# Attention behind a mixture of experts: the first batch's maxima are transposed twice, and plain scores run five slots ahead instead of nine

## What is computed

```python
xn = _layernorm(x)
x = x + attention(xn) + moe(xn)          # B=8, S=256, E=256

# attention: 16 heads of 16, with rotary q and k
scores = jnp.einsum('bshd,bthd->bhst', q, k) / jnp.sqrt(D)
scores = jnp.where(causal, -jnp.inf, scores)
attn = jax.nn.softmax(scores, axis=-1)
out = jnp.einsum('bhst,bthd->bshd', attn, v).reshape(B, S, E) @ Wo + bo

# moe: 64 experts, the best 6 of each token, and 2 shared ones
routed = jnp.einsum('tef,ehf->th', silu(g) * u * comb, w_down)
```

## Time and profile before

| | us |
|---|---|
| Runs of the kernel before, three | 647.65, 649.49, 653.19 |
| Their median | 649.49 |
| The profiled execution | 650.96 |
| Span of its trace, first to last instruction | 649.1 |
| TensorE busy, share of the span | 615.3, 95% |
| VectorE / ScalarE / GpSimd busy | 430.5 / 307.2 / 321.0 |

### The profile page before, as it was taken

How to read it: one execution, slowest core, us unless ns; L and a number is a source line. 1 busy time by engine, 2 the same in 40 slices (tenths; PEclk the granted TensorE clock), 3 DMA queues, 4 the chain that set the end, 5 groups by cost and what they waited for, 6 DMA issues and landing times.

```text
span 649.1 us, 17796 instructions
## 1 busy us (share of the span) xinstructions
PE 615.3 (95%) x4929; PEld 364.3 (56%) x4929; DVE 430.5 (66%) x1366; ACT 307.2 (47%) x802; POOL 321.0 (49%) x340
## 2 busy tenths in 40 slices
PE   6999999998998999998999999999999899999987
PEld 3644455654554555554555555555554566666654
DVE  6768688557664665667665565544446788899865
ACT  3643131033443444444444544444445777777752
POOL 4000000268636775567765686564300776766662
PEclk9999999999997999999999999999999999999999
DMA  9610011138978768996799977996425777777432
GB/s 297 179 30 2 0 34 34 57 103 255 283 228 278 232 190 247 320 334 185 213 298 295 315 222 235 327 327 134 102 59 193 210 232 229 227 227 232 129 109 74
DMA packets 78167, 124.52 MB, mean 192 GB/s; under 512 B 11113, under 2 KB 52618, under 8 KB 78090
## 3 DMA queue, kind: packets, MB, share of 16 engines
q1 hardware_dynamic: 43098, 60.18, 30.4%
q0 software_dynamic: 15872, 46.16, 24.4%
q10 hardware_dynamic: 19120, 17.18, 7.8%
HBM read 85.73 MB, written 37.75 MB: 190 GB/s over the span
## 4 chain that ended last, share of the span: by engine, by line
PE 80%; DVE 6%; DMA 3%; issue 3%; ACT 3%; POOL 2%; DVEq 1%; SPq 0%; ACTq 0%; POOLq 0%
PE pair L1216 23%; PE pair L1243 14%; PE pair L1186 6%; PE pair L1173 5%; PE pair L1121 4%; PE bank L1227 4%; PE bank L1330 4%; PE bank L1200 3%; PE bank L1362 2%; PE pair L1083 2%; DVE negm L985 2%; DMA lower<-xn_rows,idx_all 2%; PE pair L1292 2%; PE pair L1312 1%; PE bank L1341 1%
## 5 line engine op out<-in xcount | busy, mean ns | idle before, releaser
L454 POOL DMA_INDIRECT lower<-xn_rows,idx_all x128 | 138.0, 1078 | 221.8 <-DVE idx_all L958 107.8
L1216 PE MATMUL pair<-space,work 128*64 (+1 forms) x768 | 167.4, 467 | 6.3 <-DVE wqkv_sb L932 3.7
L1243 PE MATMUL pair<-lower,work 88*64 x512 | 121.5, 379 | 0.7 <-ACT lower L615 0.7
L1216 PEld LDWEIGHTS pair<-space,work 128*64 128x64 f32 x768 | 67.4, 138 | 78.4 <-issue 66.9
L874 DVE TENSOR_TENSOR work<-work,pair 128x176 f32<-128x176 f32 x128 | 42.9, 337 | 101.5 <-ACT work L609 100.7
L1243 PEld LDWEIGHTS pair<-lower,work 88*64 88x64 f32 x512 | 69.6, 137 | 48.7 <-issue 18.0
L1216 PE MATMUL pair<-wqkv_sb,work 128*64 128x352 f32 x256 | 90.6, 477 | 0.0
L615 ACT ACTIVATE lower<-pair 128x256 f32<-128x256 f32 x128 | 49.1, 384 | 76.5 <-PE pair L1243 76.5
L519 POOL DMA_INDIRECT wqkv_sb<-y_rows,slot_i x48 | 48.1, 1002 | 58.2 <-DVE negm L985 33.2
L602 ACT ACTIVATE work<-pair 128x256 f32<-128x256 f32 x128 | 42.6, 381 | 66.9 <-PE pair L1173 41.3
L985 DVE TENSOR_REDUCE negm<-pair 128x2 f32<-128x256 f32 (+1 forms) x128 | 64.6, 549 | 9.5 <-PE pair L1292 7.5
(11 more groups left out here) (205 smaller groups left out, 1156.5 us busy)
## 6 DMA issues: line engine op xcount, KB each, us to landing
space<-wgu SPq DMA_DIRECT2D x66, 352.0 KB
y_rows<-lower ACTq DMA_DIRECT2D x128, 128.0 KB, 4.3
qk_all<-qk_rows SPq DMA_DIRECT2D x64, 256.0 KB
lower<-wdn SPq DMA_DIRECT2D x64, 176.0 KB
qk_rows<-qk_all POOLq DMA_DIRECT2D x32, 256.0 KB, 5.7
qk_rows<-space POOLq DMA_DIRECT2D x16, 256.0 KB, 4.0
xn_rows<-qk_all SPq DMA_DIRECT2D x16, 128.0 KB, 1.9
lower<-xn_rows,idx_all POOLq DMA_INDIRECT x128
```

What stands on the lines that cost most here:

```text
L454: po.indirect_dma_start(xg[:, r % XB, :], None, xn_rows[:, :], bass.IndirectOffsetOnAxis(idx_all[:, r:r + 1], 0)).then_inc(xg_in[r % XB], 16)
L1216: last = pe.matmul(pair[u % 2][strip, 0:2 * F], xgT[u][:, c, strip], n, start=c == 0, stop=c == EC - 1, skip_group_check=True)
L1243: last = pe.matmul(pair[u % 2][strip, 512:512 + E], hT[:, u % 2, c, strip], n, start=c == 0, stop=c == 1, skip_group_check=True)
```

## The change

A new constant EARLY = 5. Plain scores run five slots ahead of slot 0; slots 0 to 3 make two each, and from slot 4 on the distance is AHEAD = 9 as before. Ring copies run two further ahead than the scores, and follow the same pattern. The first batch's maxima are turned twice: version 0 of mT holds those of pairs 0 to 3 and serves slots 0 to 3; version 1, made in slots 1 to 3, holds all eight and serves slots 4 to 7; later batches' versions are numbered one higher. halves(0) stands behind the maxima of pair 3, halves(1) behind those of pair 7. negm is cleared at the start. POOL's rows and the constants AHEAD, FILL and LATER are as before.

```diff
+EARLY = 5
+        def scored_at(n):
+            if n < 0:
+                return range(max(n + EARLY, 0), n + EARLY + 1)
+            return range(EARLY + 2 * n, EARLY + 2 * n + 2) if n < EARLY - 1 else range(n + AHEAD, min(n + AHEAD + 1, NS))
+        def ringed_at(n):
+            if n < 0:
+                return range(max(n + EARLY + 2, 0), n + EARLY + 3)
+            return range(EARLY + 2 + 2 * n, EARLY + 4 + 2 * n) if n < EARLY - 1 else range(n + FILL, min(n + FILL + 1, NS))
+        def version_at(n):
+            if n == EARLY - 2:
+                return 1
+            return 0 if n == -1 else (n + 1) // 8 + 1 if n % 8 == 7 and 0 < (n + 1) // 8 < B else None
+        def version_of(n):
+            return n // PAIRS_OF_HEADS + 1 if n >= EARLY - 1 else 0
...
             def a_slot(n):
                 if 0 <= n < NS:
                     exps(n)
-                if n % 8 == 7 and 0 <= (n + 1) // 8 < B:
-                    mT_copy((n + 1) // 8)
+                if version_at(n) is not None:
+                    mT_copy(version_at(n))
                 if n % 8 == 7 and 0 <= (n - 3) // 2 < QUADS:
                     raw_copy((n - 3) // 2)
-                if 0 <= n + FILL < NS:
-                    ring_copy(n + FILL)
+                for f in ringed_at(n):
+                    ring_copy(f)
...
             def d_slot(n):
-                if 0 <= n + AHEAD < NS:
-                    maxes(n + AHEAD)
+                for m in scored_at(n):
+                    maxes(m)
+                    if m == EARLY - 2:
+                        halves(0)
+                    elif m == PAIRS_OF_HEADS - 1:
+                        halves(1)
...
-                if n % 8 == 6 and 0 <= (n + 2) // 8 < B:
-                    halves((n + 2) // 8)
+                if n > 0 and n % 8 == 6 and (n + 2) // 8 < B:
+                    halves((n + 2) // 8 + 1)
...
             dve.memset(npad[:], 0.0)
+            dve.memset(negm[:], 0.0)
...
             def p_slot(n):
-                if 0 <= n + AHEAD < NS:
-                    score_masks(n + AHEAD)
+                early = scored_at(n)
+                for m in early[:1]:
+                    score_masks(m)
                     if n < 0:
-                        keep_on(bank[2][:], 3 if n + AHEAD == 0 else 1)
-                    scores(n + AHEAD)
+                        keep_on(bank[2][:], 3 if m == 0 else 1)
+                    scores(m)
                 if 0 <= n < NS:
                     turned_masks(n)
                     if n == 0:
                         keep_on(bank[2][:], 4)
                     turned_scores(n)
+                for m in early[1:]:
+                    score_masks(m)
+                    scores(m)
```

More of the change, by code:

```diff
@@ L981, in maxes @@
                 dve.wait_ge(s_ok, m + 1)
-                if m and m % PAIRS_OF_HEADS == 0:
-                    dve.wait_ge(npad_ok, m // PAIRS_OF_HEADS)
+                if m == EARLY - 1:
+                    dve.wait_ge(npad_ok, 1)
+                elif m and m % PAIRS_OF_HEADS == 0:
+                    dve.wait_ge(npad_ok, m // PAIRS_OF_HEADS + 1)
                 for qt in range(SB):
@@ L989, in halves @@
             def halves(b):
-                dve.wait_ge(max_ok, PAIRS_OF_HEADS * (b + 1))
+                dve.wait_ge(max_ok, PAIRS_OF_HEADS * b if b else EARLY - 1)
                 if b:
@@ L1307, in turned_scores @@
             def turned_scores(n):
-                b, x = n // PAIRS_OF_HEADS, n % PAIRS_OF_HEADS
-                pe.wait_ge(mT_ok, b + 1)
+                v, x = version_of(n), n % PAIRS_OF_HEADS
+                pe.wait_ge(mT_ok, v + 1)
                 q, k = ring[:, n % RING, 0], ring[:, n % RING, 1]
                 for j in range(2):
-                    pe.matmul(pair[1][:, 512 * j:512 * j + SPAN], pick[own[j], x], mT[own[j], b % 2],
+                    pe.matmul(pair[1][:, 512 * j:512 * j + SPAN], pick[own[j], x], mT[own[j], v % 2],
                               start=False, stop=False, skip_group_check=True)
@@ L1376, in p_slot @@
                     turned_scores(n)
+                for m in early[1:]:
+                    score_masks(m)
+                    scores(m)
                 w = n // 2 - 1
[L1378 to L1382, removed]
+                v = version_at(n)
+                if v is not None:
+                    if v > 1:
+                        pe.wait_ge(on_ok, NG * (v - 2) + 2)
+                    m_transpose(v)
                 if NS <= n < NS + 6:
@@ L1394, in p_slot @@
                     elif (w - 1) % NG == 2:
-                        pe.wait_ge(mT_ok, min((w - 1) // NG + 2, B))
+                        pe.wait_ge(mT_ok, min((w - 1) // NG + 3, B + 1))
                     elif w == 1:
-                        pe.wait_ge(mT_ok, 1)
+                        pe.wait_ge(mT_ok, 2)
                     back(w - 1)
```

## The result

The changed kernel takes 653.76 us (median of 20 runs, 647.34 to 657.42) against 649.14 for the kernel before (20 runs beside them, 645.84 to 653.19). The medians differ by 4.6 us. The ratio, which leaves out the one run of the changed kernel that was over 1.5% above its fastest, is 1.0051, 95% interval 1.0031 to 1.0070: 3.3 us slower, 2.0 to 4.5. That is inside the range on record and of the sign of the forecast, and less than the one per cent that the prediction set for telling a change from none, but it is more than the +1.96 us of the sum. The run left out, 657.42 us (span 655.6), is the profiled one.

The account below looks back on a forecast made before the run. Slot 7's transpose was taken to hang on the first gather, released by the eighth maximum. The −4.32 us start is lost in the catch-up and +1.96 reaches the end: 649.49 median to 651.5 us, range 648.0 to 655.0.

Parts of the forecast that it names:

- sign of the forecast: Whole kernel: slower than before, +1 to +3.8 us (650.5 to 653.3), chance 0.62.
- one per cent: Whole kernel: 6.5 us, about what a measurement can tell from no change; faster 0.02, same 0.94, slower 0.04.
- +1.96 us of the sum: Whole kernel: the eighth maximum's delay goes through gather, combine, halves and transpose to the end, +1.96 us, giving 651.5 us.
- Prologue: Ahead of slot 0: four maxima instead of eight, so everything hanging on them, slot 0's softmax included, comes 4.32 us earlier.
- Catch-up, the deciding step: Slot 7's plain scores wait for a ring copy queued behind slot 0's softmax; eighth maximum at 504.30, 1.96 us later.
- lower bound: Eighth maximum if the ring copy were free: VectorE alone needs until 502.62, still 0.28 us late.
- rival priced at +0.28: Catch-up: the ring copy isn't waited for, +0.28 us; part of little or nothing moves (649.8 to 650.2), chance 0.14.
- Gathers, combine, transpose: Behind the eighth maximum: all shift by 1.96 us; first gather 505.13, first combine 515.35, slot 7's transpose 520.56.
- Landing of the sixth gather: From the sixth gather's issue to its data: taken as unchanged at 3.96 us, called uncertain, −1.2 to +1.8.
- rival with a heavier queue: Two ring loads per turn among the gathers delay them: +3.8 to +5 us, 653.3 to 654.5, chance 0.12.
- Slots 0 to 3: Doubled plain scores: 2.45 us a loop against 1.60; of 4.32 us only 0.38 left by slot 4's softmax.
- TensorE's clock: Attention stage: granted 1.00 in all stretches, so no charge for the longer wait at 518.6.

Follow-up runs that it names:

- ring kernel: Changed kernel with its ring copies two pairs further ahead, gathers as in the change: 652.06 us, ratio 1.0046 to the kernel before.
- Late gathers: Kernel before with only its first three gathers waiting for one maximum more: 650.43 us, ratio 1.0044 to the kernel before.
- early gathers: Changed kernel with its first gathers waiting for the first maximum only: 648.56 us, ratio 0.9992 to the kernel before.
- fillers: Changed kernel with four filler matmuls on TensorE ahead of slot 7's transpose: 652.50 us, ratio 1.0063 to the kernel before.
- last experiment: All gathers four slots earlier in the kernel before (647.34 us), the changed kernel (647.62) and the changed kernel with ring copies two further ahead (646.43).

## Why the prediction was right and where it was wrong

**Prologue: right.** Slot 0's softmax was forecast at 501.28; less the 2.03 us by which this execution was late already, it stood at 501.29.

**Catch-up, the deciding step: right.** ScalarE's ring copies stand behind the softmax, TensorE waits for them (0.88), and the eighth maximum ends at 504.23 (less 2.03) where 504.30 was forecast. The ring kernel confirms that wait and shows its size: with the copies further ahead it is gone and the maximum comes 0.59 us sooner. The lower bound was too low. With ring copies that nobody waits for, the prediction had the eighth maximum 0.28 later than before; in the ring kernel it stays 9.72 − 8.42 = 1.30 later. VectorE waits there 1.03 us for pair 6's plain scores (row at 499.46), as in the changed kernel (row at 503.73), because in slot 0 they stand on TensorE behind the turned scores. 0.28 + 1.03 = 1.31. So the ring copy is the wait that ends last, as forecast, but without it only 0.59 of the 1.89 us go; the order in the doubled slot holds most of the rest, and the rival priced at +0.28 was priced too low.

**Gathers, combine, transpose: right, and shown from both sides.** First gather 505.06 (forecast 505.13), combine 515.42 (515.35), wait 3.28 (about 3.3), transpose 520.55 (520.56). Late gathers alone rebuild the delay in the kernel before; early gathers alone take the wait at the combine out of the changed kernel. At equal clock the step is worth +1.1 ± 0.6 in the runs by the common line (+1.8 by the changed kernel's own), +1.95 in the trace.

**Landing of the sixth gather: near enough here, but not a constant.** Taken as unchanged at 3.96; the transfer took 4.08, and the combine followed its issue by 517.45 − 513.34 = 4.11. In the other kernels this last distance was 3.51 (ring), 3.70 (late gathers) and 4.72 (fillers), which is why single stamps behind the combine differ by about a microsecond between kernels. None is near the 2.3 us estimated from the Trainium skill (DMA: Bandwidth & Descriptors, "Anatomy of one DMA — SWDGE (gpsimd) path"). The rival with a heavier queue is thereby excluded as the cause of the missing time: it asked for +1.8 to +3 and got 4.08 − 3.96 = +0.12.

**Slots 0 to 3: right.** 2.46 us for slot 0 against 2.45; slot 4's softmax 17.74 from the first reduction against 18.09, so 0.35 left of 4.3, forecast 0.38. The last experiment shows that this loop, and not the reduction of eight maxima, eats the start.

**TensorE's clock: wrong, and the step that failed.** The prediction said that there was "no charge for the longer wait at 518.6", because the clock had been 1.00 in every stretch of before, in one of which TensorE idled 2.0 of 13.00 us. That was read from a sum of idle time over a stretch, whose waits near the transpose were 0.55 us and less; it said nothing on a wait of 2 us. The stretches were those of the attention alone; earlier in the same trace 190 to 215 us stood at 0.86, and TensorE's timeline has there:

```profile
203.43 0.69 PE L1173 MATMUL pair<-id_f,lower 128*128 128x128 f32 x2 [2.46 <-DMA lower<-xn_rows,idx_all]
```

So the trace of before already showed a fall of the clock beside a wait of over 2 us, and the term was put at nothing without looking there. Measured in the changed kernel: 0.51 for 6 us, up to 2.55 us late (some 2.1 if the 0.43 of the late-gather kernel comes without the clock), and a mean clock of 0.9905 against 0.9961 over the runs. With this term the sum for an execution like the profiled one is 1.95 + 2.55 = +4.5; it need not happen in each (one run of the changed kernel took 647.34 us at a mean clock of 0.997, 3 thousandths below full, and a fall such as this takes 4.5), and the runs give +3.3.

The Trainium skill, TensorE: Matmul & The Clock Gate, "A second HAM failure mode: psum-queue depth-cycling", tells of a kernel in which short idle times between groups of matmuls came often enough for the clock to swing between its two levels. This case agrees in so far as the falls at slot 7's transpose stand behind groups of waits (0.47, 0.43 and 2.11; 1.13, 0.43 and 2.11; 1.10, 0.43 and 0.91) and none behind the lone 2.16. It doesn't bear this out throughout: the ring kernel lost its clock at 151 us behind a lone wait of 1.54.

**Open.** In which executions the clock falls. The kernel with late gathers kept it through 2.16 us, the changed kernel with early gathers lost it at 498 us behind 0.49 us, the ring kernel lost it at 151 us behind 1.54 us. That the waits ahead of the transpose bring the fall about is what the mean clocks of the kernels point to; it was not shown by taking one of them away alone, since the attempt with fillers came too late. Nor is it shown that the lower clock in 140 to 165 us is the whole of the 2.03 us by which the profiled execution was late before the attention. It fits that in the ten profiled executions the first reduction stood between 488.96 and 495.95, earliest in the two without any fall ahead of it (488.96 and 490.11).

## What to carry to other kernels

When the start of a pipelined stage is shortened, look up every semaphore that paces something else by a count of that prologue: here six gathers followed the eighth maximum one behind the other, and they, not the softmax, held the end. Work that is taken out of a prologue comes back in the first turns of the loop, so cost the longer turns against the start that is won (four turns of 2.45 instead of 1.60 us ate 3.4 of 4.3). And where a forecast makes the engine that sets the pace wait longer, give its clock a price of its own, from the mean clock of several runs, look through the whole trace for places where it fell, and don't read its absence from a stretch without such a wait.

## What the runs showed of the hardware that was not expected

- A fall of TensorE's granted clock to 0.51 behind a wait can cost more than the wait: some 2.1 to 2.55 us for 6 us at that level, behind a wait of 2.11 us that had made the transpose 1.95 us late. Behind a wait of 2.16 us in another kernel the clock held, behind one of 1.54 us with none close ahead of it, it fell.
- The same order of waits kept the clock in one execution (0.47 us at 500.69, 1.00) and lost it in another (0.49 us at 497.96, 0.50 to 0.60), and the mean clock of single runs of the kernel before lies between 0.990 and 1.000 with 0.53 us to each thousandth by the common line: most of the spread of its runs.
- The sixth gather of 128 rows (128 KB) is used 3.5 to 4.7 us after its issue where VectorE waits for it (3.51, 3.70, 4.11, 4.72), in kernels whose instructions around it hardly differ.
